# Output row pairs placed over 128 partitions, with the rows of even blocks brought together by ScalarE, in a batched bilinear interaction kernel

## The reference

```python
r_feature: (2048, 200, 64) fp32        # batch, fields, embedding
weight:    (200, 64, 64) fp32          # one 64x64 matrix for each field
bilinear = einsum('bie,ied->bid', feature, weight)
out      = einsum('bid,bjd->bij', bilinear, feature)     # (2048, 200, 200) fp32
```

## Time and profile before

| | |
|---|---|
| median of 3 runs | 1464.77 us (1463.12 to 1466.21) |
| the profiled execution, its own time | 1466.7 us |
| its span, first to last instruction | 1464.8 us |
| TensorE busy / weight loads busy | 1402.8 / 1219.5 us |
| VectorE busy | 1167.1 us |
| ScalarE busy | 831.2 us |
| GpSimd busy (its queue's stores) | 294.9 us |
| mean granted TensorE clock | 0.998 |
| DMA | 438.58 MB, 299 GB/s |

### The profile page before, as it was taken

How to read it: one execution, slowest core, us unless ns; L and a number is a source line. 1 busy time by engine, 2 the same in 40 slices (tenths; PEclk the granted TensorE clock), 3 DMA queues, 4 the chain that set the end, 5 groups by cost and what they waited for, 6 DMA issues and landing times.

```text
span 1464.8 us, 40028 instructions
## 1 busy us (share of the span) xinstructions
PE 1402.8 (96%) x16192; PEld 1219.5 (83%) x16192; DVE 1167.1 (80%) x2048; ACT 831.2 (57%) x929; POOL 294.9 (20%) x518
## 2 busy tenths in 40 slices
PE   6999999999999999999999999999999999999975
PEld 5888888888888888888888888888888888888854
DVE  0578878788887888878887788877888788887897
ACT  4565565656655566555655556555565555655532
POOL 0112222122122222222221122212222122221222
PEclk9999999999999999999999999999999999999999
DMA  9899999999999999999999999999999999999898
GB/s 221 248 301 292 312 314 301 315 295 310 313 310 300 298 308 314 307 307 296 311 298 309 317 294 307 320 308 300 293 308 306 317 314 292 319 302 314 254 274 260
DMA packets 280918, 438.58 MB, mean 299 GB/s; under 512 B 53408, under 2 KB 252064, under 8 KB 280736
## 3 DMA queue, kind: packets, MB, share of 16 engines
q1 hardware_dynamic: 256160, 422.79, 89.8%
q0 software_dynamic: 24576, 13.24, 6.2%
HBM read 108.13 MB, written 327.68 MB: 298 GB/s over the span
## 4 chain that ended last, share of the span: by engine, by line
PE 77%; DVE 16%; issue 4%; DMA 2%; SPq 0%; ACT 0%; POOLq 0%
PE ps L236 41%; PE made L220 23%; PE made L204 12%; DVE staging L266 8%; DVE win L316 4%; DVE win L323 3%; DMA x<-feature_dram 2%; DVE win L324 1%; PE ps L220 0%; PE ps L204 0%; SPq L149 0%; ACT bl L290 0%; SPq L142 0%; POOLq L60 0%; POOLq L133 0%
## 5 line engine op out<-in xcount | busy, mean ns | idle before, releaser
L236 PE MATMUL ps<-win,bl 64*100 64x200 f32 x8192 | 841.4, 345 | 39.2 <-DVE staging L266 39.1
L236 PEld LDWEIGHTS ps<-win,bl 64*100 64x100 f32 x8192 | 702.3, 207 | 131.8 <-issue 60.5
L266 DVE COPY staging<-ps 100x800 f32<-100x800 f32 x512 | 503.5, 983 | 200.6 <-PE ps L236 200.2
L266 ACT COPY staging<-ps 100x800 f32<-100x800 f32 x512 | 423.6, 827 | 368.2 <-PE ps L236 368.2
L186 POOL DMA_DIRECT2D out_dram<-staging x512 | 294.2, 575 | 1161.7 <-ACT staging L266 879.8
L220 PE MATMUL made<-xt,w 64*64 64x128 f32 x6000 | 369.9, 272 | 0.0
L220 PEld LDWEIGHTS made<-xt,w 64*64 64x64 f32 x6000 | 322.7, 133 | 42.7 <-issue 42.7
L316 DVE COPY win<-xt 128x400 f32<-128x400 f32 x512 | 275.4, 538 | 65.7 <-ACT xt L280 49.9
L290 ACT COPY bl<-made 128x1024 f32<-128x1024 f32 (+1 forms) x195 | 191.2, 980 | 195.2 <-PE made L220 195.2
L204 PE MATMUL made<-ident,x 128*128 128x128 f32 x1552 | 214.6, 281 | 10.1 <-DMA x<-feature_dram 9.1
L280 ACT COPY xt<-made 128x1024 f32<-128x1024 f32 (+1 forms) x202 | 198.2, 981 | 44.3 <-PE made L204 44.3
(11 more groups left out here) (5 smaller groups left out, 0.6 us busy)
## 6 DMA issues: line engine op xcount, KB each, us to landing
out_dram<-staging SPq DMA_DIRECT2D x1024, 300.0 KB, 5.7
x<-feature_dram SPq DMA_DIRECT2D x192, 512.0 KB, 6.4
out_dram<-staging POOLq DMA_DIRECT2D x512, 25.0 KB, 5.2
x<-feature_dram SPq DMA_DIRECT2D x16, 256.0 KB, 5.2
w<-weight_dram SPq DMA_DIRECT2D x24, 128.0 KB, 6.8
w<-weight_dram SPq DMA_DIRECT2D x2, 64.0 KB, 5.1
```

The lines of the kernel that those rows point to most:

```text
L236: last = nc.tensor.matmul(ps[s % TILES][0:FH, h, F * b:F * (b + 1)], rows_of_bl(n, R * k + PB * i + b)[64 * h:64 * h + 64], win[64 * h:64 ...
L266: copy(staging[:, slot, :, :, :].rearrange("p b h j -> p h b j"), ps[s % TILES][0:FH, :, 0:PB * F].rearrange("p h (b j) -> p h b j", j=F)) ...
```

## The change

- Where a pair m stands on an axis of `bl` and on the partitions of the output is now given by `places`: pairs 0 to 63 on even places, 64 to 95 on places 1, 5, 9 and so on, 96 to 99 on places 3, 7, 11 and 15. Batch entries are placed by the same rule on the other axis.
- The weights of a scores matmul have 128 columns in place of 100, so `ps` and `staging` have 128 partitions, of which 28 hold nothing that is stored. GpSimd clears the places 100 to 127 of `bl` once.
- In even blocks ScalarE copies, for each quad, its four rows of `bl` to the new tensor `rows` (`fill_rows`, 128x512, read at steps of 512 B, written contiguously), and the matmuls take their weights from there. It does so after the `stage` of each even set, two quads ahead; for quads 0 and 1 of an even block at sets 60 and 62 of the block ahead, and in block 0 before the first scores. `rows` has three slots.
- `store_bl` is two copies of half the size. The first writes at a step of 8 B in even blocks. The second writes at a step of 16 B in even blocks. In odd blocks both write runs of 8 elements, at a step of 8 B for groups 0 to 7 and 16 B for groups 8 to 12.
- SP stores the 64 even places of each set, and the 32 places 1, 5, 9 and so on of two sets at once. The GpSimd queue stores the last four places as before.
- `staging` has ten slots in place of twelve.

The core of the diff:

```diff
-    OSLOTS = 12
+    OSLOTS = 10
+    RSLOTS = 3
+    EVENS = 64
-    FA = FH // 16 * 16
+    FA = 96
...
+        rows = sbuf("rows", [128, RSLOTS, R, NB])
-        staging = sbuf("staging", [FH, OSLOTS, PB, 2, F])
+        staging = sbuf("staging", [NB, OSLOTS, PB, 2, F])
...
+        def places(number, count=1):
+            if number < EVENS:
+                return slice(2 * number, 2 * (number + count) - 1, 2)
+            if number < FA:
+                return slice(4 * (number - EVENS) + 1, 4 * (number + count - EVENS) - 2, 4)
+            return slice(4 * (number - FA) + 3, 4 * (number + count - FA), 4)
+
         def group_of_bl(n, u):
+
+            at = places(8 * u, GROUPS[u])
             if n % 2 == 0:
-                return bl[:, 8 * u:8 * u + GROUPS[u], :]
-            return bl[:, :, 8 * u:8 * u + GROUPS[u]]
-
-        def rows_of_bl(n, b):
-            return bl[:, 0:FH, b] if n % 2 == 0 else bl[:, b, 0:FH]
+                return bl[:, at, 0:NB:2], bl[:, at, 1:NB:2].rearrange("p c (g j) -> p c j g", j=2)
+            return bl[:, 0:NB:2, at], bl[:, 1:NB:2, at].rearrange("p (g j) c -> p j g c", j=2)
+
+        def quad_of_bl(n, k):
+            assert n % 2 == 0
+            return bl[:, :, places(R * k, R)].rearrange("p m r -> p r m")
+
+        def row_of_bl(n, b):
+            if n % 2:
+                return bl[:, places(b).start, :]
+            return rows[:, (n // 2 * QUADS + b // R) % RSLOTS, b % R, :]
...
-                sp.dma_start(out_v[0:FA, PB * s:PB * (s + 1), :], staging[0:FA, slot]
-                             ).then_inc(out_written[slot], 16)
+                sp.dma_start(out_v[0:EVENS, PB * s:PB * (s + 1), :], staging[places(0, EVENS), slot]
+                             ).then_inc(evens_written[slot], 16)
+                if s % 2:
+                    wait_staged(sp, s - 1)
+                    sp.dma_start(out_v[EVENS:FA, PB * (s - 1):PB * (s + 1), :],
+                                 staging[places(EVENS, FA - EVENS), slot - 1:slot + 1].rearrange("p s b h j -> p (s b) (h j)")
+                                 ).then_inc(odds_written[slot // 2], 16)
...
+            nc.gpsimd.memset(bl[:, places(FH, NB - FH), :], 0.0).then_inc(bl_cleared, 1)
...
+                    if n % 2 == 0:
+                        pe.wait_ge(rows_filled, n // 2 * QUADS + k + 1)
...
-                        last = nc.tensor.matmul(ps[s % TILES][0:FH, h, F * b:F * (b + 1)],
-                                                rows_of_bl(n, R * k + PB * i + b)[64 * h:64 * h + 64],
+                        last = nc.tensor.matmul(ps[s % TILES][:, h, F * b:F * (b + 1)],
+                                                row_of_bl(n, R * k + PB * i + b)[64 * h:64 * h + 64],
...
-                nc.scalar.copy(group_of_bl(n, u), rows.rearrange(cells, b=NB)).then_inc(bl_stored, 1)
+                weighed = weighed.rearrange("p (c b) -> p c b", b=NB)
+                low, high = group_of_bl(n, u)
+                order = ("p c b -> p c b", "p c (j g) -> p c j g") if n % 2 == 0 else ("p c b -> p b c", "p c (j g) -> p j g c")
+                nc.scalar.copy(low, weighed[:, :, 0:EVENS].rearrange(order[0]))
+                nc.scalar.copy(high, weighed[:, :, EVENS:NB].rearrange(order[1], j=2)).then_inc(bl_stored, 1)
+
+            def fill_rows(n, k):
+                q = n // 2 * QUADS + k
+                if k == 0:
+                    act.wait_ge(bl_stored, (n + 1) * NG)
+                    if n == 0:
+                        act.wait_ge(bl_cleared, 1)
+                if q >= RSLOTS:
+
+                    before = q - RSLOTS
+                    act.wait_ge(scores_done, 2 * (before // QUADS * 2 * QUADS + before % QUADS) + 2)
+                nc.scalar.copy(rows[:, q % RSLOTS], quad_of_bl(n, k)).then_inc(rows_filled, 1)
...
+            for k in range(RSLOTS - 1):
+                fill_rows(0, k)
...
                         stage(act, nc.scalar.copy, staged_act, n * SETS_B + s)
+                        k = s // 2 + RSLOTS - 1
+                        if n % 2 == 0 and k < QUADS:
+                            fill_rows(n, k)
+                        elif n % 2 and n + 1 < BLOCKS and k >= QUADS:
+                            fill_rows(n + 1, k - QUADS)
```

More of the change, by code:

```diff
@@ L39, in feature_interaction @@
     TILES = 3
-    OSLOTS = 12
+    OSLOTS = 10
     WSLOTS = 4
-    FA = FH // 16 * 16
+    RSLOTS = 3
+    EVENS = 64
+    FA = 96
     assert 2 * E == 128 and B % NB == 0 and FH % 8 == C and R == 2 * PB
-    assert PB * F <= 512 and OSLOTS % 2 == 0
+    assert PB * F <= 512 and OSLOTS % 2 == 0 and FA < FH <= NB
     feature_v = feature.rearrange("b f e -> b (f e)")
@@ L87, in feature_interaction @@
         bl_stored = sem("bl_stored")
+        bl_cleared = sem("bl_cleared")
+        rows_filled = sem("rows_filled")
         own_filled = sem("own_filled")
@@ L92, in feature_interaction @@
         staged_dve = sem("staged_dve")
-        out_written = [sem(f"out_written{i}") for i in range(OSLOTS)]
+        evens_written = [sem(f"evens_written{i}") for i in range(OSLOTS)]
+        odds_written = [sem(f"odds_written{i}") for i in range(OSLOTS // 2)]
         rest_written = [sem(f"rest_written{i}") for i in range(OSLOTS // 2)]
@@ L169, in _ @@
                 uses = (BLOCKS * SETS_B - slot + OSLOTS - 1) // OSLOTS
-                sp.wait_ge(out_written[slot], 16 * uses)
+                sp.wait_ge(evens_written[slot], 16 * uses)
                 if slot % 2:
+                    sp.wait_ge(odds_written[slot // 2], 16 * uses)
                     sp.wait_ge(rest_written[slot // 2], 16 * uses)
@@ L186, in store_rest @@
                 nc.gpsimd.dma_start(out_v[FA:FH, PB * (s - 1):PB * (s + 1), :],
-                                    staging[FA:FH, slot - 1:slot + 1].rearrange("p s b h j -> p (s b) (h j)")
+                                    staging[places(FA, FH - FA), slot - 1:slot + 1].rearrange("p s b h j -> p (s b) (h j)")
                                     ).then_inc(rest_written[slot // 2], 16)
@@ L263, in stage @@
             if used:
-                engine.wait_ge(out_written[slot], 16 * used)
+                engine.wait_ge(evens_written[slot], 16 * used)
+                engine.wait_ge(odds_written[slot // 2], 16 * used)
                 engine.wait_ge(rest_written[slot // 2], 16 * used)
             copy(staging[:, slot, :, :, :].rearrange("p b h j -> p h b j"),
-                 ps[s % TILES][0:FH, :, 0:PB * F].rearrange("p h (b j) -> p h b j", j=F)
+                 ps[s % TILES][:, :, 0:PB * F].rearrange("p h (b j) -> p h b j", j=F)
                  ).then_inc(staged, 1)
@@ L287, in store_bl @@
                     act.wait_ge(scores_done, (n - 1) * SETS_B + 4 * u + GROUPS[u] // 2)
-                cells = "p (c b) -> p c b" if n % 2 == 0 else "p (c b) -> p b c"
-                rows = bilinear_tile(n, u)[:].rearrange("p a c -> p (a c)")[:, 0:NB * GROUPS[u]]
-                nc.scalar.copy(group_of_bl(n, u), rows.rearrange(cells, b=NB)).then_inc(bl_stored, 1)
+                weighed = bilinear_tile(n, u)[:].rearrange("p a c -> p (a c)")[:, 0:NB * GROUPS[u]]
+                weighed = weighed.rearrange("p (c b) -> p c b", b=NB)
[13 more added lines that the diff above has]
+                nc.scalar.copy(rows[:, q % RSLOTS], quad_of_bl(n, k)).then_inc(rows_filled, 1)
             store_xt(0)
```

## The result

The changed kernel took 1512.3 us (median of four runs, 1511.5 to 1518.1) against 1464.5 for the kernel before: a ratio of 1.0335, with a 95% interval of 1.0323 to 1.0348. The forecast was 1495.3 within 1453 to 1532, slower, with the fills of `rows` as the cause. The direction and that cause held; the size was short by 17 us. Of the 47.7 us that the kernel lost, 30.5 were forecast.

A forecast was written before the change was run, and what follows sets the result against it. TensorE was taken to bound the kernel, VectorE where scores come alone, and DMA nowhere; -19.4 + 9.9 + 37.8 + 2.2 = +30.5 us on 1466.7 gave 1497.2, or 1495.3 at the median's level, within 1453 to 1532.

The forecast's parts named there:

- Spreading 0, with 0 to -3 us at the end: Output spread over partitions: no copy waited for a store, so only the last stores could gain; taken as 0.
- the issue price of 317 ns: SP's cheapest store issue; three for two sets were put at 0.95 us, hidden behind 2.30 us or more.
- Strided weights gone, -19.4: Even-block bursts lose the 512 B step of their weight loads: 22 bursts x 8 blocks x 0.11 us.
- 128 columns, +9.9: Weight loads 23 ns longer make each burst 0.03 us longer: 22 bursts x 15 blocks.
- The count of 22 bursts in a block: 11 periods of two bursts per block in which a change on TensorE's path was taken to reach the end.
- Filling `rows`, +37.8: In even blocks a 1.03 us fill delays `store_xt`, so TensorE waits 0.43 us: 11 periods x 8 blocks.
- The step that was off is the time that TensorE takes to go on, 0.15 us: TensorE's delay after a ScalarE copy, taken off the 0.42 us between `store_xt` and the bilinear in the fill term.
- The count of 11 a block: Periods per even block in which TensorE was forecast to wait 0.43 us for `store_xt` behind a fill.
- the third rival: Strided writes from a 16 B step cost as reads: `store_bl` waits add 20.8 us (odd), 22.7 (even), 1539 us; chance 0.13.
- no price: First rival: ScalarE reads SBUF at any step as fast as PSUM, fill 0.59 us, -7.7, 1457 us; chance 0.27.
- Ahead of the first scores, +2.2: At the start, first scores wait for the next block's `store_xt` and the first fill: 55.70 against 53.46 us.
- Ten slots, 0 to +5: Slot pairs reused after 10.3 us against 8.3 us slowest landing; taken as 0, a few us at most.

The follow-up runs named there:

- the run with both edits: Changed kernel with fills reading contiguous elements of `w` and `bl` in plain order (wrong weights, output rows misplaced): 1453.5 us, ratio 0.993.
- the third such kernel: Kernel before with 100-place fills behind `store_xt` and `store_bl`, twelve slots, three of x, fills reading two neighbouring entries at each place: 1456.3 us.

## Why the prediction was right where it was, and where it wasn't

- **What bounds.** Right: TensorE and the waits between it and ScalarE for `made`, VectorE in the scores-only stretches (block 15 takes 72.1 us as before), no waits for stores to speak of.
- **Spreading 0, with 0 to -3 us at the end.** The range was right: -2.7 us in the profiles, and the end took 5.5 to 7.0 us in seven profiles with spread stores, 7.9 to 8.7 in the three with one store of 96 in which no staging copy waited. I took the zero though, and the issue price of 317 ns was wrong for these stores, as told above. The term's reason, that nothing waited for a store, was true of the stores of before only; the cut into 64 and 32 needs the spreading.
- **Strided weights gone, -19.4, and 128 columns, +9.9.** Weight loads are at 186 ns as worked out, bursts at 1.56 us. With nothing else in the way (both steps mended) even blocks went from 90.2 to 87.9 us and odd ones from 87.2 to 87.9, and blocks 0 to 14 together took 11.0 us less, where the two terms say 9.5. The count of 22 bursts in a block was low: 26 are in the twelve periods (as the run with 128 strided columns shows), and 26 x 0.03 = 0.78 us fits what the odd block grew by. In the kernel with 128 columns alone an odd block grew by only 0.4 us; why it is 0.8 in the others stays open.
- **Filling `rows`, +37.8.** The mechanism and the place were right. The fill took 1.11 us for the 1.03 worked out from TensorE's loads, and ScalarE's neighbours overlap more, by 0.10 us (634.10 + 1.11 against 635.11 in the timeline), than the 0.06 read from the start; that nearly evens out. The read cost 28.4 us beside the slow writes and 32.0 without them. Most waits came to 0.33 us for 0.43 (1.89 us from the burst's start to the bilinear's, less 1.56). The step that was off is the time that TensorE takes to go on, 0.15 us: it was read ahead of transposes, and there it is 0.14 (680.58 to 680.72), but ahead of the bilinear it is 0.04 (636.14 to 636.18). With 0.04 the margin is 0.41 us, and the sum for the wait gives 0.32. The count of 11 a block was near in effect and not in kind: nine waits, three of them 0.6 to 0.7 us long. In groups 9 to 11 the other wait stands in its place.
- **Writes at a step of 16 B: the term that was left at zero.** This is the step that failed. The forecast priced both halves of `store_bl` at 0.59 us, from rows in which each write fills its 16 B (runs of 8 elements or more), and left the rest to the third rival with a chance of 0.13. The rival's price of the copy (1.03 for 1.09) and its wait in odd blocks (0.27 for 0.29) were right, its counts were not. In odd blocks nine periods have the wait, not eleven: where four sets stand between a bilinear and the next transposes, `store_bl` has time. That is 7 x 2.4 = 17 us for 20.8. In even blocks it added 0.71 us for four groups on top of the fill's wait, 22.7 us. In fact three groups have a wait, of 0.64 us, and it takes the place of the fill's 0.33; an even block is 1.1 us longer than with the writes mended (93.1 and 92.0), 9 us in all. So the writes cost 26.7 us in place of 43.5, and the kernel came out between the forecast and the rival. The same argument that priced the read from TensorE's loads, by elements of SBUF that lie apart, held for writes; giving it 0.73 for reads (all but no price) and 0.13 for writes was inconsistent.
- **Ahead of the first scores, +2.2.** The wait for the first fill is there, 2.1 us, but the first staging copy starts at 54.2 us as before (54.5). In the other runs it starts between 51.1 and 58.5 us, and that spread covers the term.
- **Ten slots, 0 to +5.** 1.6 us.

The sum, step by step: without the two steps of 16 B and more the forecast's terms are -19.4 + 9.9 + 2.2 = -7.3, with the measured end -10.0 us; the run with both edits stood 9.8 below the kernel before. That they meet so closely is in part luck, since the +2.2 does not show in its start (53.6 us for 54.5) and its blocks gained 11.0 us, not 9.5. The read's step added 32.0 (forecast 37.8) and the write's 26.7 (forecast 0), 58.7 in all: 58.7 - 9.8 = 48.9, less the 1.2 us by which the kernel before stood lower beside that run, is the 47.7 measured.

## What to carry to other kernels

Before a layout is changed for one reader's sake, go through all engines that read or write it, and look at the innermost step of each access: one fp32 element to each 16 B of SBUF cost nearly double here, and another loop order with two to each 16 B cost next to nothing (0.62 us against 0.59). A copy added to an engine that is 57% busy is not free by that share; what counts is whether it stands ahead of a copy that another engine waits for. Moving it behind that copy brought 24 us with no other edit.

## What was not expected of the hardware

- ScalarE's copy of 512 fp32 elements took 0.59 us from PSUM to contiguous SBUF, read contiguously or at a step of 512 B, 0.62 from contiguous SBUF, 1.11 from SBUF at a step of 512 B, and 1.04 to 1.09 to SBUF at a step of 16 B.
- A TensorE weight load of 64 partitions x 100 columns took 163 ns contiguous, 167 at 8 B and 252 at 512 B.
- Stores cut into partitions 0 to 63 and 64 to 95 cost 117 us (1605.7 against 1488.2) over one store of 0 to 95 with the same rows. Up to about 32 us of it is TensorE's granted clock, which fell after the waits.
- With TensorE's path 3 us shorter in each even block, unspread stores hold up staging copies for 15 to 18 us whether there are ten slots or twelve (3.8 us in the fastest execution of the third such kernel), and runs spread over 9 to 12 us, where the kernel before has 3 to 4. With spread partitions the kernel with both steps mended had no such wait, at blocks of 87.9 us for 87.1 to 87.5. Whether spreading could pay there, if it came without its slow writes, wasn't tried.
